# Mixture-of-experts stage: tokens of experts three to eight read by indirect DMA, and one weight chunk fewer split in two parts

## The reference, cut to what matters

```python
cap = int(CF * T / NE)                       # 1.2 * 625 / 8 = 93 tokens for an expert
probs = softmax(xf @ gate_w.T + gate_b)
topw, topi = top_k(probs, 2)
sel_w, sel_idx = top_k(wm.T, cap)            # for each expert its 93 tokens and their weights
xg = xf[sel_idx]                             # (8, 93, 512)
h = gelu(einsum('ecd,edh->ech', xg, w1) + b1)        # 512 -> 2048, exact gelu
out = einsum('ech,ehd->ecd', h, w2) + b2             # 2048 -> 512
of = zeros.at[sel_idx].add(out * sel_w)
x = x + of
```

## Time and profile before

| | us |
|---|---|
| median of 3 runs (2091.36 to 2091.61) | 2091.52 |
| span of the profiled execution, first to last instruction | 2089.1 |
| first product of the first expert (e = 0) to first product of the second (e = 1) | 177.7 to 206.0 |
| the experts e = 1 to 7 | 206.0 to 397.7 |
| everything behind them | 397.7 to 2089.1 |

### The profile page before, as it was taken

How to read it: one execution, slowest core, us unless ns; L and a number is a source line. 1 busy time by engine, 2 the same in 40 slices (tenths; PEclk the granted TensorE clock), 3 DMA queues, 4 the chain that set the end, 5 groups by cost and what they waited for, 6 DMA issues and landing times.

```text
span 2089.1 us, 36144 instructions
## 1 busy us (share of the span) xinstructions
PE 2070.5 (99%) x13385; PEld 1945.4 (93%) x13385; DVE 1501.9 (72%) x3088; ACT 1139.8 (55%) x3030; POOL 881.8 (42%) x707
## 2 busy tenths in 40 slices
PE   8999999999999999999999999999999999999998
PEld 7986666788899999999999999999999999999997
DVE  8779998844667667777767776677777677766776
ACT  4566777524755445555555554455555555544564
POOL 0010001201655545555555555455555555554461
PEclk9999999999999999999999999999999999999999
DMA  5205999900421111111122211211111222121110
GB/s 141 96 16 180 327 333 322 313 7 9 141 74 65 65 65 65 65 65 65 65 82 93 84 66 65 65 65 65 65 65 65 80 97 82 66 65 65 61 46 25
DMA packets 89161, 201.15 MB, mean 96 GB/s; under 512 B 8196, under 2 KB 12580, under 8 KB 88985
## 3 DMA queue, kind: packets, MB, share of 16 engines
q1 hardware_dynamic: 86746, 196.28, 27.6%
q0 software_dynamic: 2240, 2.57, 0.5%
HBM read 196.31 MB, written 2.51 MB: 95 GB/s over the span
## 4 chain that ended last, share of the span: by engine, by line
PE 95%; DVE 4%; ACT 1%; DMA 0%; issue 0%; POOL 0%; SPq 0%; DVEq 0%
PE PS L54 85%; PE PS L53 6%; PE PS L57 4%; DVE LW L60 1%; DVE JU L76 1%; DMA X<-in_x 0%; DVE OHsx L68 0%; DVE ACC L60 0%; DVE SM L107 0%; DVE XFL L60 0%; DVE OHdx L69 0%; DVE PO L68 0%; DVE U L69 0%; DVE W1L L60 0%; ACT UH L88 0%
## 5 line engine op out<-in xcount | busy, mean ns | idle before, releaser
L54 PE MATMUL PS<-ZH,WS 128*128 128x314 f32 x4096 | 946.5, 311 | 0.0
L54 PEld LDWEIGHTS PS<-ZH,WS 128*128 128x128 f32 x4096 | 692.2, 189 | 0.0
L54 PE MATMUL PS<-ZL,WS 128*128 128x314 f32 x2048 | 626.1, 306 | 0.0
L60 DVE TENSOR_TENSOR ACC<-ACC,PS 128x314 f32<-128x314 f32 x1008 | 476.1, 477 | 196.9 <-PE PS L54 186.9
L54 PEld LDWEIGHTS PS<-ZL,WS 128*128 128x128 f32 x2048 | 387.7, 189 | 0.0
L60 POOL TENSOR_TENSOR WS<-RAW,WS 128x512 fp32r<-128x512 f32 x256 | 327.0, 1298 | 116.6 <-ACT WS L88 116.6
L60 POOL TENSOR_TENSOR ZS<-ZS,ZQ 128x628 f32<-128x628 f32 x128 | 198.5, 1551 | 231.3 <-ACT ZQ L88 231.1
L60 POOL TENSOR_TENSOR ML<-MF,MH 128x400 fp32r<-128x400 f32 x124 | 130.4, 1052 | 346.7 <-ACT MH L88 346.7
L88 ACT ACTIVATE ZH<-PS,g1T 128x628 fp32r<-128x628 f32 x128 | 100.6, 786 | 314.8 <-PE PS L54 314.8
L88 ACT ACTIVATE EE<-EE,SM 125x100 f32<-125x100 f32 x640 | 233.0, 376 | 1.2 <-DVE SM L68 1.2
L88 ACT ACTIVATE MF<-PS 128x400 f32<-128x400 f32 x128 | 64.7, 506 | 303.1 <-PE PS L53 302.4
(11 more groups left out here) (366 smaller groups left out, 3589.2 us busy)
## 6 DMA issues: line engine op xcount, KB each, us to landing
RAW<-in_L_ffn_wz_w SPq DMA_DIRECT2D x66, 1024.0 KB, 6.2
RAW<-in_L_ffn_w SPq DMA_DIRECT2D x64, 1024.0 KB, 7.2
RAW<-in_L_ffn_Wq_w SPq DMA_DIRECT2D x32, 1024.0 KB, 8.5
CB<-c_rows SPq DMA_DIRECT2D x32, 195.3 KB
RAW<-in_L_gnn_W SPq DMA_DIRECT2D x4, 1024.0 KB, 16.1
RAW<-in_L_ffn_Wkv_w SPq DMA_DIRECT2D x4, 1024.0 KB, 14.6
RAW<-in_L_ffn_Wk_T SPq DMA_DIRECT2D x2, 1024.0 KB, 18.6
WB<-w_rows SPq DMA_DIRECT2D x6, 273.4 KB
```

The costliest lines, as they stand in the source:

```text
L54: return self.q.matmul(o, l, r, start=start, stop=stop)
L60: return Nothing() if self.q is None else self.q.tensor_tensor(out=o, in0=a, in1=b, op=op)
```

## The change

- **Tokens.** While the first expert is prepared, SP writes the normed tokens `MU` to memory (`x_rows`, 626 rows of 2 KB, row 0 zeros). `WSP` gets two more columns, each token's row number and zeros. For e = 2 to 7 PE no longer forms the ten products with `XFH` and `XFL`. Five products with `WSP` (four columns instead of two) stand behind up 1 of the expert before, in bank 4 (`places_of`); DVE copies the row numbers as integers to `IX`, and POOL issues one indirect DMA of 94 rows from `x_rows` into `XG`, two buffers in the place of `XFL`. `gathered_T` transposes `XG` once that DMA has landed. The copy to `OT` on ACT falls away for these experts.
- **Weights.** `split(m)` is m % 8 < 6 for all experts: chunks 6 and 7 of every expert go to PE as float32. n is 6e, and each expert has six calls of `weights` instead of seven. The two parts of the third quarter of the gelu output are no longer written.
- **Waits.** The first write of `GEH` waits for the write of `x_rows` (it lies over `MU`); the first gelu of an expert waits for PE's use of the chunk 6 before it; POOL's `YL` gathers wait for the landing of the last `XG`.

```diff
-        NB = 6
+        NB, NP_ = 6, 2
+        xrow = nc.dram_tensor("x_rows", (626, D), f32, kind="Internal").ap()
...
-            return m % 8 < (7 if m < 8 * NE - 8 else 6)
+            return m % 8 < 6
...
+            q.dma(xrow[0:1, :], ZR[:, :]).then_inc(s_wrow, 16)
+            q.wait_ge(*xfh_done.of(4, "u"))
+            for lo, hi in ((0, 120), (120, 125)):
+                q.dma(xrow[1:626, :].rearrange("(t p) d -> p t d", p=P)[lo:hi], MU[lo:hi, :, :]).then_inc(s_wrow, 16)
...
+            q.wait_ge(s_wrow, 80)
+            for e in range(NP_, NE):
+                q.wait_ge(*sw_v.of(e, "row"))
+                q.wait_ge(*(xg_t.of(e - 2) if e >= NP_ + 2 else ga_mm.of(NP_ - 1)))
+                if e > NP_:
+                    q.wait_ge(s_rows, 16 * (e - NP_))
+                q.gather(XG[:, e % 2, :], xrow, IX[:, e % 2:e % 2 + 1]).then_inc(s_rows, 16)
...
+            def places_of(e):
+                k = e % 2
+                q.wait_ge(*rank_v.of(e, "po"))
+                q.wait_ge(*gate_v.of("wsl"))
+                q.wait_ge(*mconst.of("code"))
+                q.wait_ge(*free[4])
+                for t in range(T5):
+                    i = q.mm(PS[0:CS, 4, 0:4], PO2[:, k, t, :], WSP[:, t, e, :], t == 0, t == 4)
+                i.then_inc(*sw_mm.up(e))
+                free[4] = sw_v.of(e, "two")
...
+                    q.wait_ge(s_rows, 16 * (e - NP_ + 1))
                 q.wait_ge(*free[b])
+                rows = OT[:, :] if e < NP_ else XG[:, e % 2, :]
```

More of the change, by code:

```diff
@@ L1174, in program @@
         YH = at("YH", [P, T5, D], f32, after("HW3"))
+        XG = at("XG", [CS, 2, D], f32, after("XFH"))
+        IX = at("IX", [CS, 2], i32, after("XG"))
         LG = at("LG", [P, T5, 8], f32, after("XFL"))
@@ L1177, in program @@
         WM = at("WM", [P, T5, 8], f32, after("GS"))
-        WSP = at("WSP", [P, T5, 8, 2], f32r, after("WM"))
+        WSP = at("WSP", [P, T5, 8, 4], f32r, after("WM"))
         RKA = at("RKA", [P, 8, T5], f32, after("WSP"))
@@ L1183, in program @@
         IH = at("IH", [P, T5], i32, after("IL"))
-        c4 = at("c4", [P, 2, T5, 64], f32, after("IH"))
+        TOK = at("TOK", [P, T5], f32, after("IH"))
+        c4 = at("c4", [P, 2, T5, 64], f32, after("TOK"))
         CD = [at(f"CD{k}", [P, 6, T5], f32, after("IH") + 128 * k) for k in range(3)]
@@ L1322, in g_moe @@
             q.fill(io94[:, CAP:CS], -1.0).then_inc(*mconst.up("all"))
+            q.wait_ge(*mconst.of("all"))
+            q.iota(TOK[:, :], [[P, T5]], 1).then_inc(*mconst.up("token"))
+            q.wait_ge(*mconst.of("token"))
+            q.ts(WSP[:, :, :, 2], TOK[:, :].unsqueeze(2).broadcast_to([P, T5, 8]), 1.0, None, ALU.add)
+            q.fill(WSP[:, :, :, 3].bitcast(f32), 0.0).then_inc(*mconst.up("code"))
             q.wait_ge(*x1_done.of(4))
@@ L1359, in weights @@
                     c = slice(1024 * h, 1024 * h + 1024)
-                    q.act(HW[(i + 1) % 4][:, c], raw[:, c], ACT.Copy).then_inc(*w_hi.up(m, h))
+                    q.act(HW[i % 4][:, c], raw[:, c], ACT.Copy).then_inc(*w_hi.up(m, h))
             for i in range(2):
@@ L1398, in dispatch @@
                     q.act(PT[:, k, 500:625], PS[0:CS, 5, 0:P], ACT.Copy).then_inc(*pt_done.up(e))
-                q.wait_ge(*ga_mm.of(e))
-                q.act(OT[:, :], PS[0:CS, 6, :], ACT.Copy).then_inc(*ga_done.up(e))
+                if e < NP_:
+                    q.wait_ge(*ga_mm.of(e))
+                    q.act(OT[:, :], PS[0:CS, 6, :], ACT.Copy).then_inc(*ga_done.up(e))
             def gathered_T(e):
@@ L1577, in rank_end @@
                 if e >= 2:
-                    q.wait_ge(*ga_mm.of(e - 2))
+                    q.wait_ge(*sw_mm.of(e - 2))
+                    if e - 2 < NP_:
+                        q.wait_ge(*ga_mm.of(e - 2))
+                    if e - 2 >= NB:
+                        q.wait_ge(*pt_t.of(e - 2))
                 for t in range(T5):
@@ L1592, in dispatch @@
                     q.wait_ge(*os_hi.of(e - 2))
-                q.cp(sw[k][:, 0:2], PS[0:CS, 7, 0:2]).then_inc(*sw_v.up(e, "two"))
+                b = 7 if e < NP_ else 4
+                if e >= NP_:
+                    if e > NP_ + 1:
+                        q.wait_ge(s_rows, 16 * (e - NP_ - 1))
+                    q.cp(IX[:, k:k + 1], PS[0:CS, b, 2:3]).then_inc(*sw_v.up(e, "row"))
+                q.cp(sw[k][:, 0:2], PS[0:CS, b, 0:2]).then_inc(*sw_v.up(e, "two"))
                 q.wait_ge(*sw_v.of(e, "two"))
@@ L1808, in dispatch @@
                 for t in range(T5):
[L1809 removed]
+                    i = q.mm(PS[0:CS, 7, 0:2], PO2[:, k, t, :], WSP[:, t, e, 0:2], t == 0, t == 4)
                 i.then_inc(*sw_mm.up(e))
                 free[7] = sw_v.of(e, "two")
+            def places_of(e):
[8 more added lines that the diff above has]
+                free[4] = sw_v.of(e, "two")
             def gathered_T(e):
                 b = xg_bank(e)
[L1815 removed]
+                if e < NP_:
+                    q.wait_ge(*ga_done.of(e))
+                else:
+                    q.wait_ge(s_rows, 16 * (e - NP_ + 1))
                 q.wait_ge(*free[b])
+                rows = OT[:, :] if e < NP_ else XG[:, e % 2, :]
                 for f in range(4):
[L1818 removed]
+                    i = q.tr(PS[:, b, CS * f:CS * f + CS], rows[:, 128 * f:128 * f + 128], ident[0:CS, 0:CS])
                 i.then_inc(*xg_t.up(e))
@@ L1966, in a_counts @@
         def a_counts(q):
-            q.wait_ge(*w_used.of(chunk(7 * NE - 4)))
+            q.wait_ge(*w_used.of(8 * NE - 5))
             for m in range(T5):
@@ L1972, in v_counts @@
             for m in range(T5):
-                q.wait_ge(*w_used.of(chunk(7 * NE - (3 if m < 4 else 2))))
+                q.wait_ge(*w_used.of(8 * NE - (4 if m < 4 else 3)))
                 q.wait_ge(*gch_done.of(m))
```

52 lines of the change are left out of this document (27 added, 25 removed).

## The result

| | us |
|---|---|
| before, median of 5 runs (2090.95 to 2091.61) | 2091.36 |
| after, median of 5 runs (2103.24 to 2104.58) | 2103.35 |
| ratio, with its 95% interval | 1.0057, 1.0046 to 1.0068 |
| span of the profiled execution, before and after | 2089.1 and 2101.5 |

What follows compares the result with a forecast made beforehand. The prediction took PE to bound six experts, with little room in the DMA engines. From 2091.5 us it took 10.2 for PE, added 0.9 of DMA waiting and 0.4 at the end: 2082.6 us, range 2080.8 to 2089.5.

Steps and rivals of the forecast that it cites:

- the write of the tokens: SP's write of 1.3 MB ahead of the first chunk load: 3.8 us, costing nothing unless it took three times as long.
- PE's own sum: PE in the experts' stage: -13.9 us of removed products, +3.9 and -0.2 for chunk 6 in float32, together -10.2 us.
- Part 3: Less work for ACT and DVE in each expert: neither becomes the bound by its work; worth nothing more in itself.
- Part 6: The gather into XG lands 9.1 us after issue, with 13.0 us available, so it costs nothing; range end 1.4 us per expert.
- The late gather: Rival: PE waits in gathered_T for XG; gain gone at a 14.7 us landing, 2099.3 us at 16 us; chance 0.10.
- Part 5: DMA engines: a gather takes 1.3 us, engines fall behind 0.4 us per expert, so PE waits about 0.9 us in all.
- the prediction's gap of 2.6 us: Idle time of the DMA engines in one expert before the change: 2.6 us, or 1.4 if a share of 1.00 is full.
- Part 4: ACT's queue: chunk 3 is wanted ahead of the XGH copy; its landing can hold XGH, XGL and PE; slack 1.4 us.
- 2087.3 for the queue: Rival: the DMA queue becomes the bound in the experts' stage, 2087.3 us with the worse ends; chance 0.25 for 2084.5 to 2090.
- Part 7: Around the stage: token write costs nothing; at the end X<-X,YH has 1.5 us of slack; 0.4 us taken (0 to 1.5).

Runs made afterwards that it cites:

- nogather: The changed kernel with each gather into XG replaced by a GpSimd fill of zeros; 2081.1 us, ratio 0.9950 to before.
- n96y: The changed kernel with XG gathers of 96 rows instead of 94 and the ten YL and YH gathers of 128 instead of 125; 2081.6 us, repeated 2084.3.
- n96: The changed kernel with XG gathers of 96 rows instead of 94; 2085.5 us, ratio 0.9972 to before.
- by128: The kernel before with the ten gathers of results (YL, YH) of 128 rows instead of 125; 2091.0 us, ratio 0.9995.
- g94_s7: The changed kernel's token part alone, with 94-row gathers and seven chunks split as before; 2103.7 us, ratio 1.0062 to before.
- g96_s7: The changed kernel's token part alone, with 96-row gathers and seven chunks split as before; 2087.9 us, ratio 0.9984 to before.

## Why the prediction was wrong

**What held.** The second expert starts at 205.5 us instead of 206.0, so the write of the tokens cost nothing. PE's own sum, -10.2 us, came out as -10.4 without the transfers (nogather), and chunk 6 in float32, +3.7, as +3.3 alone. Part 3 held too. An expert of 25.6 us is what n96y shows when little waits: 25.5 to 26.1 us over e = 1 to 6, first and last row here, in the columns of the stretches above:

```profile
205.50:231.00 25.50, 25.50 (x115) 15.98 (x114) 22.57 (x39) 18.57 (x34) 2.70 (x1) 1.00 0.99 347
...
334.50:360.60 26.10, 26.10 (x121) 16.55 (x119) 18.41 (x34) 19.19 (x36) 9.22 (x7) 1.00 1.04 359
```

**The balance.** Products and weights -10.4; six gathers spread well +4.4 (nogather 2081.1 to n96 2085.5); the same gathers on two engines instead of sixteen +17.9 (2085.5 to 2103.4). Sum +11.9. The forecast had +1.3 for the last two together. The +4.4 is uncertain by some 3 us, as much as two runs of n96y differ.

**Part 6 failed first.** I took 9.1 us for the landing because YL's first gather was "nearest to one gather beside weight loads". It had 125 rows, five engines by E; this one has 94 and two. The number of rows looked like a size, and is a divisor. Against those six, 13.1 to 15.2 us, 125 rows landed in 9.1 to 14.4, and in by128 128 rows do in 6.1 to 10.4. The Trainium skill ("DMA: Bandwidth & Descriptors", section "Why a DMA increments its semaphore by 16 and not by 1") has the rule: the largest k up to 16 that divides the slowest dimension of both sides is the number of engines, 96 partitions going to 16 and 127 to one. The four row counts agree with it, 9.0, 11.0, 14.4 and 21.3 us for 16, 5, 2 and 1 engines. The prediction didn't weigh it, although the kernel itself cuts its other DMAs into pieces of 80, 112 or 120 rows and a rest, as in the write of `x_rows` (0 to 120, 120 to 125).

**The late gather came true, the price did not.** The rival put the turning point at 14.7 us of landing. In e = 1 to 3 the landings are 13.5, 15.0 and 13.9 us (the chain above) and these experts take 27.4, 28.0 and 26.8, about the old 27.3: at 14 us the gain is gone, as worked out. The limit lies 1 us earlier than I had it, since POOL starts at 215.48, T + 10.0, not T + 9.0. But by this mechanism alone the kernel would have come out near before. I gave it 0.10 and made it need two mishaps for a landing of 16 us; one was enough for 15.

**Part 5 carried most of the loss.** Against the kernel without transfers, from one first product with `XGH` to the next, e = 1 to 3 take 5.6 us more in all and e = 4 to 6, where chunk landings end the waits, 16.2. I took 1.3 us of all DMA engines for a gather, from the bytes that the queue moved in a stretch with gathers. That averages over 16 engines. By the landings a chunk waits for the slowest engine: the first gather delays it by 3.1 us (the gap of 5.8 above, less 2.7) where the same bytes over 16 engines delay it by at most 1.6 (4.3 less 2.7). With the prediction's gap of 2.6 us in an expert less 1.7 for the faster PE, that makes the queue fall behind by some 2 us with every expert, an estimate from one gather. Part 4 named the path (chunk 3 lands, `HW`, `XGH`, `XGL`, PE) and a slack of 1.4 us; the path stands in the chain, from e = 4 on. From there an expert takes 29.4, 32.3 and 32.7 us by its first product with `XGH`. One more reader stands in that queue than it named: at 343.83 PE waits for `PT`, which ACT copies behind the same chunk. Both rivals came true together; neither price reached the result (2087.3 for the queue, 2099.3 for late gathers), as the queue was priced with 1.4 us for a gather at the worst. This is how the loss came about with six calls of `weights`; with seven (g94_s7) the late gathers and the hold at the end cost as much.

**A wait feeds the clock.** A part of the last two experts is none of the transfers. PE is idle for 5.0 of the 28.4 us up to 345.5, and for 3.6 of the next 31.3. Behind the first idle time the granted clock has a mean of 0.90, behind the second of 0.78, where it stood at 1.00 (2.4 GHz) up to 317.1; so for part of each stretch it was at the lower level, 1.2 GHz:

```profile
345.50:355.90 10.40, 10.40 (x39) 5.74 (x39) 4.99 (x6) 4.00 (x6) 0.00 (x0) 0.90 0.54 182
376.80:388.30 11.50, 11.50 (x34) 5.78 (x34) 5.41 (x7) 3.69 (x5) 8.98 (x7) 0.78 0.97 210
```

The 37 products at 345.46 take 10.43 us; in n96y, whose clock is full, the same ones stand as

```profile
331.63 9.31 PE PS L54 x37
```

and the 32 that follow 376.77, in the kernel before, as

```profile
367.28 8.97 PE PS L54 x32
```

The first difference is 1.1 us. In the changed kernel the 32 products, the last 8 of expert e = 6 and the first 24 of the last, take 11.54 us, 2.6 more. So at least 3.7 of the 22 us are clock. No step of the prediction had that.

**Part 7.** The 1.5 us of slack at X<-X,YH were used up as said, but not in the changed kernel, where everything is late together. They count where TensorE comes to the last expert earlier than it does there: 7 us in g96_s7 and, at 372.9, in g94_s7.

## What to carry to other kernels

Before an indirect DMA takes the place of work on an engine, look at the factors of its row count: 94 rows cost 18 us more than 96 here, for two rows of padding. Price a transfer among others by what it puts on the busiest DMA engine, not by its bytes over all sixteen, since the loads beside it landed later the more rows one engine had. When a faster engine moves a stage forward, list the transfers at the stage's end: those that were hidden by 1.5 us held DVE's queue, and with it the run, by 7.

## What the runs showed of the hardware

- Landing of one indirect DMA of 2 KB rows beside weight loads: 9.0, 11.0, 14.4 and 21.3 us (medians) for 96, 95, 94 and 97 rows, 0.12 to 0.15 us for each row more on one engine, counted by E; their shares of 16 engines meanwhile were 34.9, 16.9, 11.8 and 7.6%.
- The queue serves the same bytes in different numbers of packets: from the totals less the 2240 of before, 64, 176, 400 and 800 packets for one gather of 96, 95, 94 and 97 rows. POOL's time to issue it goes the same way, from 3.05 to 4.26 us.
- A pad of three rows (125 to 128) takes the landing of the gathers of results from 11.9 to 6.8 us (medians), for 6 KB more in each.
- At a DMA share of 1.04 one expert moved 359 GB/s (n96y, 334.5 to 360.6) and another 342 (after, 232.9 to 260.9): the share doesn't tell a well used queue from a badly dealt one.
